# A second decay tile for turned and spread chunks in place of the fifth h tile, with sums three chunks behind

## The chip, the cores and the metric

The kernel runs on one core of one Trainium2 chip. Its time is the device time of one execution in microseconds. All numbers are float32.

## The reference

The kernel computes a conditioned block with two state-space scans, one forward in time and one backward (cut to what matters):

```python
B, S, D, E, N, R = (4, 1024, 512, 1024, 16, 64)
dbc = einsum('bse,re->bsr', u, Wdbc);  dlt, Bm, Cm = split(dbc, [R, R + N])
delta = softplus(einsum('bsr,er->bse', dlt, Wdt) + bdt)
dA = exp(delta[..., None] * -exp(Alog))          # decays, one per state n
dBu = delta[..., None] * Bm[:, :, None, :] * u[..., None]   # inflows
h = dA_t * h + dBu_t                             # scan over the tokens
y = einsum('ben,bn->be', h, C_t)                 # summed over the 16 states
...
y1 = silu(mx) * ssm(z1);  y2 = silu(mx) * flip(ssm(flip(z2)))
out = einsum('bse,de->bsd', y1 + y2, Wf) + bf + skip
return x + gate * out
```

`u` is z1 or z2, a projection of the normalised and modulated input. Batch, direction and channels are independent of each other. Only the scan is serial in time.

## The kernel before

A set-up part (about 250 us) normalises x, folds weights together and writes the projected dlt, B and C rows to DRAM. Then `ssm_kernel` works through 64 **units** (`NU`): 4 batches, 2 directions, 8 tiles of 128 channels. In units 0 to 7 of each sixteen the scan runs forward, in 8 to 15 backward. A unit has 16 **chunks** (c, from 0 to 15), one for each state n, and each chunk is a tile of 128 channels by 1024 tokens. q = 16 k + c numbers the chunks of the whole kernel. All engines run through the same two loops (k, then c), each in its own written order, and meet at semaphores.

A chunk takes these steps:

- ScalarE (ACT) makes the decays, exp(delta * A), at L1195.
- The inflows delta * u * B are made in one of three ways, which the letter of the chunk in `KINDS` names. For **V** and **P** chunks GpSimd (POOL) multiplies du by a broadcast row of B (L1233, tile `bst`) and the decays go to a PSUM tile, `slot[q % 2]`. For **A** chunks (turned) ACT scales the transposed du, eight tiles of 128x128 in two halves of four (`scale_half`, L1134, tile `abuf`), and TensorE (PE) transposes them back into `slot[q % 2]` (`turn_inflow`, L899). For **E** chunks (spread) PE multiplies the transposed du, `dut`, by diagonal matrices of B (`spread_inflow`, L911, two passes per matmul); ACT makes those matrices once in eight units (`make_diagonal`). For A and E the decays go to an SBUF tile, `dec`, of which there is one.
- VectorE (DVE) scans (L1325) into `hbuf[q % HR]` or, for V, into the slot in place.
- The scan is multiplied by a row of C: by DVE for V (L1330), by POOL for all others (`product`, L1238), in place in `hbuf`.
- PE sums the 16 products in PSUM tile `y` by transposing each into it, eight matmuls per chunk (`sum_chunk`, L888).

`HR` is the number of h tiles, `LAG` how many chunks behind its own step PE sums. In step q PE makes the inflow of chunk q, if it is A or E, and then the sum of chunk q - LAG:

```python
def sum_chunk(q):
    wait_product(pe, q)
...
if q >= HR:
    dve.wait_ge(summed, q - HR + 1)      # DVE, before scan q
```

Once per unit, around the border, come these: ACT copies y out (`copy_y`, L1125), then PE starts y anew with the skip terms (`skip_terms`, L881; it waits for that copy) and makes the delta product of the next unit (`delta_product`, L848). ACT turns that into softplus (L1090 to L1096), DVE finishes delta (L1259), PE projects z for the next unit (`z_part`, L859), DVE makes du in two halves (L1269), PE transposes them (`turn_du`, L930), and ACT copies them to `dut` (L1159).

Half of the units (1 to 8 of each sixteen) also compute the silu branch, **mx**: two banks of matmuls, each in two halves (`mx_part`, L869), the last half bank in step 0 of the next unit, ACT's sigmoid on each bank (L1109 to L1117), and a product of DVE (L1279). The other half (9 to 15 and 0) **gate** y: PE transposes it, DVE multiplies (L1291), and from unit 16 on PE projects a block of tokens through Wf (`project`, L969 and L974, half of it in step 15 and half in step 0 of the next unit), which DVE finishes (L1295). Units 9 to 14 have, in that place, the dlt, B and C products of later chunks (L962). In `z_step` the work for z starts at chunk 7 or, in gating units, 9.

POOL's order in each unit, from chunk 6 on, is: products 6 and 7, inflow 11, product 8, inflow 13, products 10 and 11, inflow 15, products 12 and 13, inflow 1 of the next unit, product 14, inflow 3, product 0, inflow 5, product 2, inflow 7, product 4, inflow 9.

Of the kernel before, what the change touches and what calls it, by code (L numbers as in the profile page):

```python
# [27 lines left out]
def setup_kernel(nc, t, scratch):  # L28

    with ExitStack() as ctx:  # L30
# [358 lines left out]
        def _(pe):  # L389
# [93 lines left out]
            for c in range(2):  # L483
# [3 lines left out]
KINDS = "EVEVAVAPAVAPAPAV"  # L487
SCALE_STEPS = {0: (4, 0), 2: (4, 1), 3: (6, 0), 5: (6, 1), 6: (8, 0), 7: (8, 1),
               8: (10, 0), 9: (10, 1), 10: (12, 0), 11: (12, 1), 12: (14, 0), 13: (14, 1)}
SPREAD = [n for n in range(N) if KINDS[n] == "E"]  # L490
SEQ = ET * N
HR = 5
LAG = 4
# [30 lines left out]
def ssm_kernel(nc, t, scratch):  # L524

    with ExitStack() as ctx:
# [3 lines left out]
        def sem(name):  # L530
# [7 lines left out]
        soft, ud, yrd, silu, ybuf, dec, dut = (sb(n, [P, S]) for n in (  # L538
            "soft", "ud", "yrd", "silu", "ybuf", "dec", "dut"))
# [58 lines left out]
        def has_mx(k):  # L598
            return not gates(k) and k % (2 * ET) != 0
# [235 lines left out]
        def _(pe):  # L835
# [183 lines left out]
            for k in range(NU):  # L1019
                e, zs = k % ET, z_step(k)  # L1020
                new_b = (k + 1) % ET == 0
                for c in range(N):
# [5 lines left out]
                    if c == 3 and k + 1 < NU:  # L1028
                        delta_product(k + 1)
                    if c == LAG:  # L1030
                        skip_terms(k)
                    if q >= LAG:
                        sum_chunk(q - LAG)
                    if c == 0 and k > 0 and has_mx(k - 1):
                        mx_part(k - 1, 1, range(2, DT))
# [45 lines left out]
        def _(act):  # L1081
# [71 lines left out]
            def copy_dut(k, h):  # L1153
                act.wait_ge(dut_mm, 2 * k + h + 1)
                if k > 0:
                    act.wait_ge(turned, before("AE", (k - 1) * N + SPREAD[-1] + 1))
                if k > 0:
                    act.wait_ge(scaled, len(SCALE_STEPS) * k - 1 + h)
                nc.scalar.activation(dut[:, half(h)], mb[h], ACT.Copy).then_inc(dut_ready, 1)  # L1159
# [10 lines left out]
            copy_bt(0)  # L1170
            for h in range(2):
                skip_half(0, h)
            for h in range(2):
                copy_dut(0, h)
            for i in range(len(SPREAD)):
                make_diagonal(0, i)

            for k in range(NU):
                f, zs = wtile(k), z_step(k)
                new_b = (k + 1) % ET == 0  # L1180
                for c in range(N):
# [3 lines left out]
                    if kind(q) in "AE":  # L1185
                        if before("AE", q) > 0:
                            act.wait_ge(scanned, TURNED[before("AE", q) - 1] + 1)
                        decays = dec[:]
# [8 lines left out]
                    if c == 0 and k > 0 and k % ET == 0:  # L1197
                        make_diagonal(k // ET, 1)
                    if c in SCALE_STEPS:
                        scale_half(N * k + SCALE_STEPS[c][0], SCALE_STEPS[c][1])  # L1200
# [4 lines left out]
                    if c == LAG - 1 and k > 0:  # L1205
                        copy_y(k - 1)
# [47 lines left out]
        def _(dve):  # L1254
# [55 lines left out]
            for k in range(NU):  # L1310
                zs = z_step(k)
                step = -1 if backward(k) else 1
                for c in range(N):
                    q = N * k + c
                    dve.wait_ge(decay_ready, q + 1)
                    if kind(q) in "AE":
                        dve.wait_ge(turned, before("AE", q + 1))
                        decays, inflows = dec, slot[q % 2]
# [107 lines left out]
```

## Time and profile before

| | |
|---|---|
| median of 3 runs | 3330.06 us (3326.39 to 3333.35) |
| the profiled execution | 3326.98 us |
| its span, first to last instruction | 3325.2 us |
| TensorE busy | 3021.0 us, 91% |
| VectorE busy | 3027.8 us, 91% |
| ScalarE busy | 2681.0 us, 81% |
| GpSimd busy | 2906.2 us, 87% |
| scans (VectorE, L1325) | 1024, 2264 to 2278 ns each |
| products (GpSimd, L1238) | 704, 2383 ns each |
| sums (TensorE, L888) | 8192 transposes |

The span is what the timelines below cover, and their times count from its start. Two instructions of one engine overlap by about 0.1 us in the records, so what an instruction takes of its engine's time is read from the start of one to the start of the next.

### The profile page before, as it was taken

Reading aid. Unit: us, or ns where it says so; the run is one execution under the profiler, and the core shown is the slowest. Engines: PE = TensorE matmul, PEld = TensorE weight load, DVE = VectorE, ACT = ScalarE, POOL = GpSimd, SP = SyncE. Lnnn points to the kernel's source line nnn. Section 1 sums busy time; section 2 is a strip of 40 time slices with the busy share of each in tenths; the row PEclk is TensorE's granted clock in tenths of the full one; section 3 lists DMA queues with packets and bytes.
Section 4 is the critical chain, followed back from the end, with each engine's and each line's share of the span. In section 5 each row is a group of like instructions: output and inputs, shape, how many; then the busy total and the mean of one; then the engine's idle time right before and its main releaser. Section 6 shows DMA issues by size and latency. Waiting matters only on the chain.

```text
span 3325.2 us, 54883 instructions
## 1 busy us (share of the span) xinstructions
PE 3021.0 (91%) x19924; PEld 2416.6 (73%) x19924; DVE 3027.8 (91%) x2008; ACT 2681.0 (81%) x5151; POOL 2906.2 (87%) x1288
## 2 busy tenths in 40 slices
PE   8887999889989999889999999899988989898999
PEld 5766667667767667678878776678777766677789
DVE  2829999999999999999999999999998999999994
ACT  1438999988788999987788999987877999988772
POOL 1518999999999999999998999999998999999993
PEclk9989999999999999999999999999999999999999
DMA  5765333644475343644575333645565344645453
GB/s 222 245 232 173 129 133 127 230 161 148 160 247 190 132 130 126 224 148 151 158 236 188 130 122 135 219 138 163 161 212 202 123 133 129 229 138 163 150 194 112
DMA packets 207054, 560.40 MB, mean 169 GB/s; under 512 B 20201, under 2 KB 66473, under 8 KB 202561
## 3 DMA queue, kind: packets, MB, share of 16 engines
q1 hardware_dynamic: 203424, 538.01, 48.6%
q0 software_dynamic: 2304, 16.78, 1.4%
q8 instruction: 159, 2.61, 0.3%
q10 hardware_dynamic: 1056, 2.10, 0.2%
q14 instruction: 111, 0.90, 0.1%
HBM read 476.19 MB, written 80.63 MB: 167 GB/s over the span
## 4 chain that ended last, share of the span: by engine, by line
PE 56%; ACT 20%; issue 8%; DVE 8%; POOL 1%; DVEq 0%; ACTq 0%; POOLq 0%
PE y L888 17%; PE slot L899 8%; PE mb L859 8%; ACT abuf L1134 7%; PE mb L969 6%; PE mb L869 5%; PE slot L911 5%; DVE hbuf L1325 4%; ACT dec L1195 4%; ACT slot L1195 3%; ACT soft L1090 2%; PE mb L848 2%; DVE slot L1325 2%; PE mb L962 1%; DVE delta L1259 1%
## 5 line engine op out<-in xcount | busy, mean ns | idle before, releaser
L1238 POOL TENSOR_TENSOR hbuf<-hbuf,cres 128x1024 f32<-128x1024 f32 x704 | 1666.6, 2383 | 182.9 <-DVE hbuf L1325 182.3
L1233 POOL TENSOR_TENSOR bst<-bst,du 128x1024 f32<-128x1024 f32 x512 | 1226.6, 2396 | 47.0 <-DVE du L1269 47.0
L1325 DVE TENSOR_TENSOR_SCAN hbuf<-dec,slot 128x1024 f32<-128x1024 f32 x512 | 1165.1, 2276 | 60.5 <-PE slot L911 36.8
L888 PEld LDWEIGHTS y<-ident,hbuf 128*128 128x128 f32 x8192 | 971.6, 146 | 137.9 <-issue 134.2
L888 PE MATMUL y<-ident,hbuf 128*128 128x128 f32 x8192 | 1067.9, 280 | 0.7 <-POOL hbuf L1238 0.7
L1134 ACT ACTIVATE abuf<-dut,bt 128x128 f32<-128x128 f32 x3072 | 970.9, 387 | 0.0
L1325 DVE TENSOR_TENSOR_SCAN slot<-slot,bst 128x1024 f32<-128x1024 f32 x320 | 729.0, 2278 | 43.6 <-ACT slot L1195 43.3
L1195 ACT ACTIVATE dec<-delta,par 128x1024 f32<-128x1024 f32 x512 | 584.7, 1142 | 127.3 <-DVE hbuf L1325 127.3
L1195 ACT ACTIVATE slot<-delta,par 128x1024 f32<-128x1024 f32 x512 | 566.5, 1107 | 118.5 <-DVE hbuf L1330 106.2
L899 PE MATMUL slot<-ident,abuf 128*128 128x128 f32 x3072 | 422.7, 282 | 168.1 <-ACT abuf L1134 148.2
L899 PEld LDWEIGHTS slot<-ident,abuf 128*128 128x128 f32 x3072 | 351.8, 145 | 298.8 <-ACT abuf L1134 223.5
L859 PE MATMUL mb<-xn,wzs 128*128 128x512 f32 x1008 | 478.7, 597 | 25.5 <-DVE delta L1259 15.0
L1325 DVE TENSOR_TENSOR_SCAN hbuf<-slot,bst 128x1024 f32<-128x1024 f32 x192 | 434.7, 2264 | 0.2 <-ACT slot L1195 0.2
L1330 DVE TENSOR_TENSOR hbuf<-slot,cres 128x1024 f32<-128x1024 f32 x320 | 391.9, 1225 | 11.0
L859 PEld LDWEIGHTS mb<-xn,wzs 128*128 128x128 f32 x1008 | 172.8, 191 | 156.2 <-issue 156.2
L911 PEld LDWEIGHTS slot<-diag,dut 128*128 128x128 f32 x2048 | 244.8, 194 | 30.5 <-issue 27.8
L911 PE MATMUL slot<-diag,dut 128*128 128x128 f32 x2048 | 253.6, 278 | 10.5 <-DVE hbuf L1325 5.1
L869 PE MATMUL mb<-xn,wx 128*128 128x512 f32 x512 | 240.9, 593 | 0.0
L969 PE MATMUL mb<-ybuf,wf 128*128 128x128 f32 x1504 | 177.8, 276 | 4.7 <-issue 3.8
L969 PEld LDWEIGHTS mb<-ybuf,wf 128*128 128x128 f32 x1504 | 173.2, 193 | 5.4 <-issue 4.4
L848 PE MATMUL mb<-dl,wdt 81*128 81x512 f32 x256 | 125.2, 610 | 13.7 <-DVE silu L1279 8.4
L1125 ACT ACTIVATE yrd<-y 128x1024 f32<-128x1024 f32 x64 | 64.8, 1013 | 84.1 <-PE y L888 84.0
(157 smaller groups left out, 2322.4 us busy)
## 6 DMA issues: line engine op xcount, KB each, us to landing
bst<-bc_s SPq DMA_DIRECT2D x512, 512.0 KB, 3.9
cres<-bc_s SPq DMA_DIRECT2D x128, 512.0 KB, 6.9
wzs<-wz_s SPq DMA_DIRECT2D x64, 256.0 KB, 4.1
yf_s<-yrd SPq DMA_DIRECT2D x32, 512.0 KB, 5.3
ybuf<-yf_s SPq DMA_DIRECT2D x32, 512.0 KB, 5.0
yg_s<-ybuf SPq DMA_DIRECT2D x31, 512.0 KB, 4.4
si_s<-silu SPq DMA_DIRECT2D x28, 512.0 KB, 6.1
silu<-si_s SPq DMA_DIRECT2D x28, 512.0 KB, 5.4
```

Source lines behind the costliest of these rows:

```text
L859: last = nc.tensor.matmul(z_bank(k, h), wz[:, i * P:(i + 1) * P], xn[:, h, i, :], start=(i == 0), stop=(i == DT - 1))
L869: last = nc.tensor.matmul(mb[h], wx[:, i * P:(i + 1) * P], xn[:, h, i, :], start=(i == 0), stop=(i == DT - 1))
L888: last = nc.tensor.matmul(y[:, j * P:(j + 1) * P], hbuf[:, q % HR, j * P:(j + 1) * P], ident[:], start=False, stop=(q % N == N - 1), is_tr ...
L899: last = nc.tensor.matmul(slot[q % 2][:, j * P:(j + 1) * P], abuf[:, a % 2, j * P:(j + 1) * P], ident[:], start=True, stop=True, is_transp ...
L911: last = nc.tensor.matmul(slot[q % 2][:, j * P:(j + 1) * P], dut[:, j * P:(j + 1) * P], diag[:, i, j, :], start=True, stop=True)
L969: nc.tensor.matmul(bank[:, m * P:(m + 1) * P], wf[:, e, m * P:(m + 1) * P], tokens, start=(e == 0 and m == 0), stop=False, skip_group_chec ...
L1134: last = nc.scalar.activation(abuf[:, a % 2, j * P:(j + 1) * P], dut[:, j * P:(j + 1) * P], ACT.Copy, scale=bt[:, g % 2, j, n:n + 1])
L1195: nc.scalar.activation(decays, delta[:, k % 2, :], ACT.Exp, scale=par[:, f // ET, f % ET, PA + c:PA + c + 1]).then_inc(decay_ready, 1)
L1233: nc.gpsimd.tensor_tensor(bst[:, i % BR, :], bst[:, i % BR, :], du[:, k % 2, :], ALU.mult).then_inc(pool_b, 1)
L1238: nc.gpsimd.tensor_tensor(hbuf[:, q % HR, :], hbuf[:, q % HR, :], cres[:, q % N, :], ALU.mult).then_inc(pool_prod, 1)
L1325: nc.vector.tensor_tensor_scan(h[:, ::step], decays[:, ::step], inflows[:, ::step], 0.0, ALU.mult, ALU.add).then_inc(scanned, 1)
L1330: nc.vector.tensor_tensor(hbuf[:, q % HR, :], slot[q % 2][:], cres[:, c, :], ALU.mult).then_inc(dve_prod, 1)
```

## The change

- Chunks 2 and 4 change places in `KINDS`: 2 is now turned, 4 is spread. ACT scales both halves for chunk 2 in its step 0.
- `dec` becomes two tiles. The decays of the i-th A or E chunk wait for the scan of the one two before it, not for the last.
- `HR` goes from 5 to 4 and `LAG` from 4 to 3. The memory of one h tile is the memory of the second `dec` tile.
- PE's step 3 now has the skip terms, sum 0 and then the delta product; before it had the delta product and sum 15 of the last unit, and the skip terms came in step 4, behind the turned inflow of chunk 4.
- ACT copies y straight behind decay 3, ahead of its scaling. The second diagonal of a new group of eight units is made in step 1 instead of 0.

```diff
-KINDS = "EVEVAVAPAVAPAPAV"
-SCALE_STEPS = {0: (4, 0), 2: (4, 1), 3: (6, 0), 5: (6, 1), 6: (8, 0), 7: (8, 1),
...
+KINDS = "EVAVEVAPAVAPAPAV"
+SCALE_STEPS = {0: ((2, 0), (2, 1)), 3: ((6, 0),), 5: ((6, 1),), 6: ((8, 0),), 7: ((8, 1),), 8: ((10, 0),),
...
-HR = 5
-LAG = 4
+HR = 4
+LAG = 3
+DEC = 2
...
+        dec = sb("dec", [P, DEC, S])
...
-                    if c == 3 and k + 1 < NU:
-                        delta_product(k + 1)
                     if c == LAG:
                         skip_terms(k)
                     if q >= LAG:
                         sum_chunk(q - LAG)
+                    if c == 3 and k + 1 < NU:
+                        delta_product(k + 1)
...
                     if kind(q) in "AE":
-                        if before("AE", q) > 0:
-                            act.wait_ge(scanned, TURNED[before("AE", q) - 1] + 1)
-                        decays = dec[:]
+                        i = before("AE", q)
+                        if i >= DEC:
+                            act.wait_ge(scanned, TURNED[i - DEC] + 1)
+                        decays = dec[:, i % DEC, :]
...
-                    if c == 0 and k > 0 and k % ET == 0:
+                    if c == LAG and k > 0:
+                        copy_y(k - 1)
+                    if c == 1 and k > 0 and k % ET == 0:
                         make_diagonal(k // ET, 1)
                     if c in SCALE_STEPS:
-                        scale_half(N * k + SCALE_STEPS[c][0], SCALE_STEPS[c][1])
+                        for n, h in SCALE_STEPS[c]:
+                            scale_half(N * k + n, h)
...
-                    if c == LAG - 1 and k > 0:
-                        copy_y(k - 1)
```

The numbers of the changed kernel's lines are one or two higher. The order of its instructions at a border with mx on PE, from the sum that stands in step 15 to the scan inflow of chunk 4 (`y<-ident,hbuf` x8 is the sum of one chunk, `y<-ident,ud` are the skip terms, `mb<-dl,wdt` is the delta product). Before:

```order
L888 MATMUL y<-ident,hbuf 128x128 x8
L869 MATMUL mb<-xn,wx 128x512 x2
L911 MATMUL slot<-diag,dut 128x128 x8
L888 MATMUL y<-ident,hbuf 128x128 x8
L869 MATMUL mb<-xn,wx 128x512 x2
L888 MATMUL y<-ident,hbuf 128x128 x8
L911 MATMUL slot<-diag,dut 128x128 x8
L888 MATMUL y<-ident,hbuf 128x128 x8
L848 MATMUL mb<-dl,wdt 128x512 x2
L888 MATMUL y<-ident,hbuf 128x128 x8
L899 MATMUL slot<-ident,abuf 128x128 x8
L881 MATMUL y<-ident,ud 128x128 x8
```

The change:

```order
L889 MATMUL y<-ident,hbuf 128x128 x8
L870 MATMUL mb<-xn,wx 128x512 x2
L912 MATMUL slot<-diag,dut 128x128 x8
L889 MATMUL y<-ident,hbuf 128x128 x8
L870 MATMUL mb<-xn,wx 128x512 x2
L889 MATMUL y<-ident,hbuf 128x128 x8
L900 MATMUL slot<-ident,abuf 128x128 x8
L889 MATMUL y<-ident,hbuf 128x128 x8
L882 MATMUL y<-ident,ud 128x128 x8
L889 MATMUL y<-ident,hbuf 128x128 x8
L849 MATMUL mb<-dl,wdt 128x512 x2
L912 MATMUL slot<-diag,dut 128x128 x8
```

The first sum is of chunk 11 before and of chunk 12 now, and every later one is likewise a chunk further. The turned inflow comes two sums earlier, as chunk 2's; the spread inflow of chunk 4 now stands behind the skip terms, a sum and the delta product.

On ACT at the same border, from decay 0 to the copy of y (`dec` and `slot` are decays 0, 1, 2 and 3, `abuf` x4 is the scaling of one half, `soft` the sigmoid on the second mx bank). Before:

```order
L1195 ACTIVATE dec<-delta,par 128x1024
L1134 ACTIVATE abuf<-dut,bt 128x128 x4
L1195 ACTIVATE slot<-delta,par 128x1024
L1109 ACTIVATE soft<-mb,par 128x512
L1112 ACTIVATE soft<-soft 128x512
L1114 ACTIVATE soft<-soft 128x512
L1117 ACTIVATE soft<-soft 128x512
L1195 ACTIVATE dec<-delta,par 128x1024
L1134 ACTIVATE abuf<-dut,bt 128x128 x4
L1195 ACTIVATE slot<-delta,par 128x1024
L1134 ACTIVATE abuf<-dut,bt 128x128 x4
L1125 ACTIVATE yrd<-y 128x1024
```

The change:

```order
L1197 ACTIVATE dec<-delta,par 128x1024
L1135 ACTIVATE abuf<-dut,bt 128x128 x8
L1197 ACTIVATE slot<-delta,par 128x1024
L1110 ACTIVATE soft<-mb,par 128x512
L1113 ACTIVATE soft<-soft 128x512
L1115 ACTIVATE soft<-soft 128x512
L1118 ACTIVATE soft<-soft 128x512
L1197 ACTIVATE dec<-delta,par 128x1024
L1197 ACTIVATE slot<-delta,par 128x1024
L1126 ACTIVATE yrd<-y 128x1024
L1135 ACTIVATE abuf<-dut,bt 128x128 x4
```

The scaling that stood behind decays 0 and 2 is all behind decay 0, and the copy of y is no longer behind the scaling for chunk 6. On DVE and POOL the order of the instructions is the same, since V, P and the two others keep their places but for 2 and 4, which both take a decay tile and a slot.

## Rows read from the trace of the kernel before

**Rows 1.** the page's first part: busy time and share of each engine

```profile
PE 3021.0 (91%) x19924; PEld 2416.6 (73%) x19924; DVE 3027.8 (91%) x2008; ACT 2681.0 (81%) x5151; POOL 2906.2 (87%) x1288
```

**Rows 2.** waits of DVE: us in total, times, longest

```profile
DVE slot L1325 <- ACT slot L1195: 43.3, 69, 1.7
DVE hbuf L1325 <- PE slot L911: 36.8, 36, 7.5
...
DVE hbuf L1325 <- ACT slot L1195: 17.2, 23, 1.1
```

**Rows 3.** timeline of DVE, units 21 and 22: start us, us, instruction, idle before

```profile
1202.90 2.27 DVE L1325 TENSOR_TENSOR_SCAN hbuf<-dec,slot 128x1024 f32<-128x1024 f32 x1
...
1229.33 2.29 DVE L1325 TENSOR_TENSOR_SCAN hbuf<-dec,slot 128x1024 f32<-128x1024 f32 x1
...
1241.28 2.28 DVE L1325 TENSOR_TENSOR_SCAN hbuf<-dec,slot 128x1024 f32<-128x1024 f32 x1
1243.94 2.30 DVE L1325 TENSOR_TENSOR_SCAN slot<-slot,bst 128x1024 f32<-128x1024 f32 x1 [0.39 <-ACT slot L1195]
...
1248.55 2.28 DVE L1325 TENSOR_TENSOR_SCAN hbuf<-dec,slot 128x1024 f32<-128x1024 f32 x1
```

**Rows 4.** timeline of POOL, the same stretch

```profile
1205.32 4.69 POOL L1238 TENSOR_TENSOR hbuf<-hbuf,cres 128x1024 f32<-128x1024 f32 x2 [1.43 <-DVE hbuf L1325]
...
1223.89 4.78 POOL L1238 TENSOR_TENSOR hbuf<-hbuf,cres 128x1024 f32<-128x1024 f32 x2
```

**Rows 5.** timeline of PE (matmuls), the same border

```profile
1225.57 1.88 PE L869 MATMUL mb<-xn,wx 128*128 128x512 f32 x4
1227.29 1.95 PE L911 MATMUL slot<-diag,dut 128*128 128x128 f32 x16
...
1229.95 1.88 PE L869 MATMUL mb<-xn,wx 128*128 128x512 f32 x4
...
1240.01 1.07 PE L881 MATMUL y<-ident,ud 128*128 128x128 f32 x8 [0.89 <-ACT yrd L1125]
...
1245.16 1.09 PE L899 MATMUL slot<-ident,abuf 128*128 128x128 f32 x8 [2.34 <-ACT abuf L1134]
1246.10 3.37 PE L888 MATMUL y<-ident,hbuf 128*128 128x128 f32 x16
```

**Rows 6.** timeline of ACT, the same border

```profile
1231.87 0.69 ACT L1109 ACTIVATE soft<-mb,par 128x512 f32<-128x512 f32 x1 [1.08 <-PE mb L869]
...
1234.45 1.14 ACT L1195 ACTIVATE dec<-delta,par 128x1024 f32<-128x1024 f32 x1
...
1238.87 1.00 ACT L1125 ACTIVATE yrd<-y 128x1024 f32<-128x1024 f32 x1
```

**Rows 7.** timeline of DVE, border of units 28 and 29

```profile
1607.26 2.29 DVE L1325 TENSOR_TENSOR_SCAN hbuf<-dec,slot 128x1024 f32<-128x1024 f32 x1 [0.56 <-PE slot L911]
...
1614.80 2.29 DVE L1325 TENSOR_TENSOR_SCAN hbuf<-dec,slot 128x1024 f32<-128x1024 f32 x1 [0.77 <-ACT slot L1195]
...
1620.46 2.27 DVE L1325 TENSOR_TENSOR_SCAN hbuf<-dec,slot 128x1024 f32<-128x1024 f32 x1
1623.32 2.30 DVE L1325 TENSOR_TENSOR_SCAN slot<-slot,bst 128x1024 f32<-128x1024 f32 x1 [0.59 <-ACT slot L1195]
```

**Rows 8.** timeline of POOL, the same border

```profile
1600.91 4.74 POOL L1238 TENSOR_TENSOR hbuf<-hbuf,cres 128x1024 f32<-128x1024 f32 x2
```

**Rows 9.** timeline of PE, the same border

```profile
1599.46 1.91 PE L888 MATMUL y<-ident,hbuf 128*128 128x128 f32 x16
1601.21 0.60 PE L930 MATMUL mb<-ident,du 128*128 128x128 f32 x4
...
1605.22 1.95 PE L911 MATMUL slot<-diag,dut 128*128 128x128 f32 x16
```

**Rows 10.** engines in a stretch: busy PE, PEld, DVE, ACT, POOL, PEclk, DMA, GB/s

```profile
1246.00:1251.00 5.00, 5.00 (x23) 4.04 (x22) 4.96 (x5) 4.62 (x12) 3.62 (x3) 0.66 0.36 121
```

**Rows 11.** cores: span and mean granted clock

```profile
core 0: 3325.2 us, clock 0.975
```

More of the change, by code:

```diff
@@ L484, in _ @@
                 project(1, c, ps[c % 2])
-KINDS = "EVEVAVAPAVAPAPAV"
-SCALE_STEPS = {0: (4, 0), 2: (4, 1), 3: (6, 0), 5: (6, 1), 6: (8, 0), 7: (8, 1),
-               8: (10, 0), 9: (10, 1), 10: (12, 0), 11: (12, 1), 12: (14, 0), 13: (14, 1)}
+KINDS = "EVAVEVAPAVAPAPAV"
+SCALE_STEPS = {0: ((2, 0), (2, 1)), 3: ((6, 0),), 5: ((6, 1),), 6: ((8, 0),), 7: ((8, 1),), 8: ((10, 0),),
+               9: ((10, 1),), 10: ((12, 0),), 11: ((12, 1),), 12: ((14, 0),), 13: ((14, 1),)}
 SPREAD = [n for n in range(N) if KINDS[n] == "E"]
 SEQ = ET * N
-HR = 5
-LAG = 4
+HR = 4
+LAG = 3
+DEC = 2
 DR = 2
@@ L537, in ssm_kernel @@
         delta, du = (sb(n, [P, 2, S]) for n in ("delta", "du"))
-        soft, ud, yrd, silu, ybuf, dec, dut = (sb(n, [P, S]) for n in (
-            "soft", "ud", "yrd", "silu", "ybuf", "dec", "dut"))
+        soft, ud, yrd, silu, ybuf, dut = (sb(n, [P, S]) for n in ("soft", "ud", "yrd", "silu", "ybuf", "dut"))
+        dec = sb("dec", [P, DEC, S])
         abuf = sb("abuf", [P, 2, S])
@@ L1157, in copy_dut @@
                 if k > 0:
-                    act.wait_ge(scaled, len(SCALE_STEPS) * k - 1 + h)
+                    act.wait_ge(scaled, 2 * KINDS.count("A") * k - 1 + h)
                 nc.scalar.activation(dut[:, half(h)], mb[h], ACT.Copy).then_inc(dut_ready, 1)
@@ L1170, in _ @@
             copy_bt(0)
+            make_diagonal(0, 0)
             for h in range(2):
@@ L1174, in _ @@
                 copy_dut(0, h)
-            for i in range(len(SPREAD)):
-                make_diagonal(0, i)
+            make_diagonal(0, 1)
             for k in range(NU):
@@ L1317, in _ @@
                         dve.wait_ge(turned, before("AE", q + 1))
-                        decays, inflows = dec, slot[q % 2]
+                        decays, inflows = dec[:, before("AE", q) % DEC, :], slot[q % 2]
                     else:
```

## Prediction

> **What bounds the kernel now.** I read the page first: VectorE (DVE) is busy for 91% of the span, and GpSimd (POOL) for 87% [rows 1]. Both times are in large equal pieces, so the next question is which of them waits, and for whom. The waits of DVE answer it: its two largest causes in the units are the decay factors of ScalarE (ACT) and the inflows of TensorE (PE), 97 us in all with the third row [rows 2]. No row of that view is a wait for a sum of PE. So DVE sets the pace, nearly packed, and a change can win 97 us at most by taking waits of DVE away. It can lose without such a ceiling, if it puts something late in front of DVE.
>
> The timelines show what is close behind. I take two borders between units, since the 64 units repeat them. Scan c means the scan of chunk c of a unit, and a prime is the next unit. The first border is between units 21 and 22, which have the silu branch (mx). Scan 6 starts at 1202.90 and one period later at 1248.55: 45.65 us [rows 3]. POOL picks up product 6 as soon as scan 6 is over (1205.32, after a wait of 1.43), and from there it never waits until the next product 6. In its fixed order (products 6, 7, inflow 11, product 8, inflow 13, products 10, 11, inflow 15, product 12) it reaches **product 12** nine operations later: the pair 12 and 13 starts at 1223.89, so product 12 is ready at about 1226.25 [rows 4]. That is 21 us after scan 6, in which DVE has come eight scans further, to scan 14. PE asks for that product only after the spread inflow of chunk 0', and does not wait [rows 5]. **This lag of POOL at the end of a unit is what the old distance of four chunks hides.**
>
> **The change, part by part.**
>
> *Sums three behind (LAG 4 to 3).* PE runs in order. In step 15 of a unit it now sums chunk 12 where it summed 11, and behind that sum stand the first mx half of the second bank and the spread inflow that scan 0' needs. PE finished the previous sum and began that mx half at 1225.57, so it asked at 1224.70 (a sum of eight transposes takes 0.87: sixteen take 1.75, from 1599.46 to 1601.21). Now it must wait to 1226.25. With 0.1 us for the signal: sum to 1227.22, mx half 1.72 (1225.57 to 1227.29) to 1228.94, and scan 0' starts 2.04 after its spread begins (1227.29 to 1229.33) [rows 3, 5]: 1230.97 in place of 1229.33, **+1.64**. Step 13 has the same for product 10, but only about 0.4 late at scan 14, and what follows swallows it.
>
> Units without mx (gating ones) have the stretch of PE from 1599.46 on: sums 10 and 11, a turn of du, half of a projection, the spread inflow at 1605.22 [rows 9]. Sum 11 begins there at 1600.33. Product 12 is the first of the pair that starts at 1600.91 [rows 8] and is ready at 1603.25, so sum 12 starts at 1603.35 in that place and everything behind it is 3.0 later: scan 0' at 1610.3, not 1607.26 [rows 7], **+3.0**. 32 units end the first way, and 29 the second (23 with a projection, 6 with the products for the next pair of chunks, which I count alike). Units 0 and 15 have nothing behind that sum and lose nothing. 32 x 1.64 + 29 x 3.0 = **+139 us**.
>
> *h tiles 5 to 4.* Scan q now needs sum q-4. PE makes it in step q-1, as it made q-5 before, so the condition is no tighter than the PE order just costed. Sum 14 is the nearest: product 14 ends three POOL operations, about 7.0 us, after product 12, so 2.3 us after the new scan 0', and scan 2' starts only about 6 us after scan 0' (two scans, a product and a silu half of DVE between). Nothing added.
>
> *Chunk 2 turned, chunk 4 spread; skip terms, sum and delta product ahead of it.* Before, PE turned chunk 4 and then waited for ACT's copy of y (0.89 at 1240.01) with nothing urgent behind [rows 5]. Now the skip terms wait for the copy in step 3, and behind them stand sum 0', the delta product and the spread inflow of chunk 4, which scan 4' needs. For the mx border, counted from scan 0': the mx half of PE begins at +0.62 [rows 3, 5], ACT's sigmoid starts at +2.54 and takes 2.58 (1231.87 to 1234.45) [rows 6], then decays 2 and 3 at 1.05 each, to 7.22, the copy, and the skip terms 1.14 after its start (1238.87 to 1240.01): 8.4. Skip terms 0.91, sum 0.87, delta product 1.72 (as many passes as an mx half), and 2.04 from spread to scan: **13.9**. Scan 4' stood at 11.95 (1229.33 to 1241.28) [rows 3]: **+1.95**. Product 0' ends five POOL operations after product 12, at about 6.9, and is in time. At the gating border PE itself sets the copy: from -0.25 it does sum 13 0.87, half a projection 3.58 (4.01 from 1601.21 to 1605.22 less 0.43 for the turn of du [rows 9]), its skip tile 0.44, sum 14, turn 2 and sum 15 at 0.87 each, so the copy starts at about 7.4, the skip terms at 8.55, and scan 4' at **14.1**; it stood at 13.2 (1607.26 to 1620.46) [rows 7], **+0.9**. In it the wait of 0.77 before scan 2' is gone, since a turn (0.87) replaces a spread (1.8). For the 6 units behind a product job I take +1.2, for the two behind neither +2. 32 x 1.95 + 23 x 0.9 + 6 x 1.2 + 2 x 2 = **+94 us**.
>
> *Second decay tile, scaling moved, copy of y ahead of it.* ACT no longer waits for the last scan before a decay of a turned chunk. DVE gains only where ACT was late: scan 5 came 2.66 after scan 4 behind mx units [rows 3] and 2.86 behind gating ones [rows 7]. Unhindered scans follow each other at 2.19 (2.28 less an overlap of 0.09), so 0.47 and 0.67 were lost. Now the softplus start is not queued behind the copy, and decay 5 is ready about 1 us early. 31 x 0.47 + 29 x 0.67 = **-34 us**. At the seven borders where B changes, ACT also makes diagonals and DVE waits for its slot up to 1.7 us [rows 2]; that hides partly under the new waits: **-4**. The scaling of chunk 2 (2.4 us) comes after decay 0' and is ready before PE's turn; no instruction and no DMA is added. SP's queue has the same order; its wait for the copy of y moves with the unit.
>
> The sum without the clock is 139 + 94 - 34 - 4 = **+195 us**.
>
> *TensorE's clock.* After a wait of 2.34 at 1245.16, the next sixteen transposes took 3.37 us [rows 5], 1.46 more than the 1.91 of the same shape [rows 9], and from 1246 to 1251 the granted clock was 0.66 of full speed [rows 10]: the lower level, 1.2 GHz, for 3.4 us (0.34 x 5 / 0.5), and 2.4 GHz for the rest. This is off the path now. After the change PE waits about 2.9 before sum 12 in gating units and about 3.2 before the skip terms in mx units, and both times the work behind leads straight to a scan. 61 such waits could cost 1.46 each, 89 us, or nothing. Were every unit to lose one such stretch now (3.4 us at half speed in 46), the mean clock would be 0.963; it is 0.975 [rows 11], two thirds of that. I take two thirds: **+60 us**.
>
> The Trainium skill, page "TensorE: Matmul & The Clock Gate", Part 1, says that the array's clock goes to its lower level when the engine has been idle and comes back only with sustained activity. That speaks against this change: by that rule every one of the longer waits is followed by a slow stretch, and the sum is 195 + 89. By [rows 10] the trace agrees for the one wait that I looked at closely.
>
> Sum: 3327 us of the profiled execution (span 3325.2 and 1.8 around it) + 255 = **3582 us**. That execution is 3 us below the median of the runs, 3330, which is under my error.
>
> **Rivals.**
> *Both waits, each followed by the low clock.* 3327 + 195 + 89 = 3611. For it: the wait of 2.34 is already followed by it, and the new ones are longer. Against: it could begin too late to touch the path. With the forecast it shares the mechanism.
>
> *One of the two new waits only.* If the chain to scan 4' is shorter than I add up (it runs through three engines), +139 - 34 - 4 - 22 (the waits before scan 2') gives 3406. If product 12 were in time, +94 - 38 gives 3383. Against the latter is the pair at 1223.89, whose start is bound to the end of scan 6 by POOL's nine operations.
>
> *Faster, by ACT.* If PE's sums were not late, DVE would be rid of its waits in the units: 0.39 in 31 of them [rows 3], 1.92 in 29 (0.56 + 0.77 + 0.59 [rows 7]), and some 7 us at the borders where B changes, 75 us in all: 3252. For it: all of those waits name ACT or PE's inflows [rows 2], and these are what the second tile and the swap relieve. It decides only if product 12 is ready within about 0.1 us of the time when PE reaches step 15, that is 1.6 us sooner in mx units and 3 us sooner in gating ones. POOL, 2.33 us an operation without a gap, gives no sign of that.
>
> *Nothing.* Gains and losses equal, 3320 to 3337. Only by chance.
>
> **How the numbers follow.** Forecast (3480 to 3640, likeliest 3582) 0.68; the full clock rule 0.12, inside the same range; one wait only 0.12; faster 0.06; nothing 0.02. The range 3460 to 3640 holds the first two whole. Its low end is the sum without the clock and with half of the chunk 4 term missing (3327 + 148 = 3475) and 15 us for my rounding; its high end is 3611 and half a microsecond per unit of waits that I overlooked. A measurement here can tell about 0.2%, 7 us. Faster 0.06, same 0.02, slower 0.92.
>
> **What would show it.** Right: PE waits for "POOL hbuf" before sums, some 60 times, about 1 to 3 us each (no row here has one); PE's wait for "ACT yrd" grows from 0.89 in mx units to about 3; DVE waits for "PE slot" at scans 0 and 4, its waits for "ACT slot" at scan 5 are gone; periods of about 49 to 51 us for mx units and 51 to 53 for gating ones; the mean clock is at or below 0.975. Wrong: periods under 46.5 in mx units, or a DVE wait for anything else that is larger.

## The result, and the profile after

The changed kernel takes 3575.57 us (median of 4 runs, 3574.32 to 3580.31), the kernel before 3331.22 (median of 4). The ratio is 1.0738, with a 95% interval of 1.072 to 1.0757: the change costs 244 us (248 between the two executions that the profiles show, of 3326.98 and 3574.61). The forecast was 3582, range 3460 to 3640, slower at 0.92.

The same work is done in more time. First the page's line of busy times, which answers to [rows 1]:

```profile
PE 3059.3 (86%) x19924; PEld 2399.7 (67%) x19924; DVE 3028.8 (85%) x2008; ACT 2681.1 (75%) x5151; POOL 2904.9 (81%) x1288
```

DVE, ACT and POOL are as busy as before within 2 us, and every share has fallen. PE has 38 us more; no matmul was added, and at least part of it is work that now falls into stretches of the lower clock (below). So nearly all of the loss is waiting, and as DVE set the pace, it must be in front of DVE. Its waits, by what ended them (us in total, times, longest), answer to [rows 2]:

```profile
DVE hbuf L1328 <- PE slot L912: 267.6, 91, 5.2
DVE hbuf L1328 <- issue: 46.2, 56, 1.7
...
DVE slot L1328 <- ACT slot L1197: 10.9, 12, 1.3
```

The waits for ACT's decays in `slot`, 43.3 us before, are down to 10.9. In their place DVE waits 268 us for the spread inflow, the one of chunk 0 or of chunk 4, where it waited 37. The row "issue", for which the profile names no releaser, is PE's inflow too: it is 28 waits before scan 0 of 1.05 us and 27 before scan 14 of 0.56, and scan 0 starts there 2.04 us after PE began the spread inflow (1368.06 and 1370.10 below), as it does where PE is named (1333.14 and 1335.18). What PE in turn waited for (the same view of PE; before, it had 0.7 us of the first row and 35.2 of the second):

```profile
PE y L889 <- POOL hbuf L1241: 162.3, 222, 3.2
PE y L882 <- ACT yrd L1126: 152.5, 62, 5.7
```

These are the two mechanisms of the forecast, though not all of each row: only 64 of the 222 waits for POOL are over 1 us, some 30 of about 1.3 (sum 10, in step 13 of mx units) and 28 of about 2.3 (sum 12, in step 15 of gating ones). Adding up from DVE's timeline what it was idle before each scan, by chunk, over the units 1 to 62 and the first chunks of 63, gives this table (us; "mx" are the 32 units that come behind an mx unit, "gating" the others):

| before scan | mx, before | mx, after | gating, before | gating, after |
|---|---|---|---|---|
| 0 | 0 | 29 | 22 | 118 |
| 1 and 2 | 7 | 3 | 27 | 4 |
| 4 | 0 | 99 | 0 | 59 |
| 5 | 12 | 0 | 16 | 0 |
| 14 | 0 | 16 | 0 | 2 |
| 15 | 6 | 4 | 3 | 4 |
| all | 25 | 151 | 69 | 186 |

That is 337 us after and 93 before, a difference of 244. There are some 46 more waits than before, and each costs the overlap of 0.1 us as well, so that this is the whole of the 248 between the two profiled executions.

**The border behind an mx unit.** DVE's timeline of unit 21 of the changed kernel (start, us, instruction, idle before) answers to [rows 3]:

```profile
1319.63 2.29 DVE L1328 TENSOR_TENSOR_SCAN hbuf<-dec,slot 128x1024 f32<-128x1024 f32 x1 [1.05 <-issue]
...
1335.18 2.29 DVE L1328 TENSOR_TENSOR_SCAN hbuf<-dec,slot 128x1024 f32<-128x1024 f32 x1 [3.51 <-PE slot L912]
1337.38 2.27 DVE L1328 TENSOR_TENSOR_SCAN slot<-slot,bst 128x1024 f32<-128x1024 f32 x1
...
1362.66 2.29 DVE L1328 TENSOR_TENSOR_SCAN hbuf<-dec,slot 128x1024 f32<-128x1024 f32 x1 [0.56 <-issue]
...
1370.10 2.29 DVE L1328 TENSOR_TENSOR_SCAN hbuf<-dec,slot 128x1024 f32<-128x1024 f32 x1 [1.05 <-issue]
```

and PE's of the same stretch answers to [rows 5]:

```profile
1327.98 1.59 PE L882 MATMUL y<-ident,ud 128*128 128x128 f32 x8 [3.21 <-ACT yrd L1126]
1329.36 1.91 PE L889 MATMUL y<-ident,hbuf 128*128 128x128 f32 x8
1331.06 2.24 PE L849 MATMUL mb<-dl,wdt 81*128 81x512 f32 x4
1333.14 1.95 PE L912 MATMUL slot<-diag,dut 128*128 128x128 f32 x16
...
1358.44 1.09 PE L889 MATMUL y<-ident,hbuf 128*128 128x128 f32 x8 [1.28 <-POOL hbuf L1241]
...
1365.41 1.09 PE L889 MATMUL y<-ident,hbuf 128*128 128x128 f32 x8 [0.25 <-POOL hbuf L1241]
1366.34 1.88 PE L870 MATMUL mb<-xn,wx 128*128 128x512 f32 x4
1368.06 1.95 PE L912 MATMUL slot<-diag,dut 128*128 128x128 f32 x16
```

In 1327.98 to 1335.18 the chain to scan 4 stands link by link: skip terms, sum 0, delta product, spread inflow, scan. The skip terms start 8.35 us after scan 0 (8.4 in the forecast). With 1327.98 to 1335.18 at 7.2 the chain is 1.65 longer than the 5.54 of the forecast: that is the low clock, seen in the first three rows (to the next row the skip terms take 1.38 and not 0.91, the sum 1.70 and not 0.87, the delta product 2.08 and not 1.72). The two waits for "POOL hbuf" are sums 10 (1.28, step 13) and 12 (0.25, step 15). The wait is split over two places: sum 10 already delays PE, so that little is left for sum 12. Scans 14 and 0 come late by 0.56 and 1.05. What fixes scan 0 is still product 12: from scan 6 (1341.96) to scan 0 it is 28.14 us, and the forecast had 28.07.

**The border behind a gating unit.** PE at the end of unit 28, and DVE's scans 0 and 4 of unit 29, answer to [rows 9] and [rows 7]:

```profile
1724.70 1.09 PE L889 MATMUL y<-ident,hbuf 128*128 128x128 f32 x8 [2.32 <-POOL hbuf L1241]
1725.63 0.60 PE L931 MATMUL mb<-ident,du 128*128 128x128 f32 x4
1726.06 3.74 PE L970 MATMUL mb<-ybuf,wf 128*128 128x128 f32 x32
1729.64 1.95 PE L912 MATMUL slot<-diag,dut 128*128 128x128 f32 x16
```

```profile
1731.68 2.29 DVE L1328 TENSOR_TENSOR_SCAN hbuf<-dec,slot 128x1024 f32<-128x1024 f32 x1 [3.55 <-PE slot L912]
...
1745.83 2.29 DVE L1328 TENSOR_TENSOR_SCAN hbuf<-dec,slot 128x1024 f32<-128x1024 f32 x1 [1.75 <-PE slot L912]
```

Scan 4 is 14.15 us after scan 0; the forecast had 14.1. The pair of products that begins with product 12 starts at 1722.29 on POOL, so sum 12 can start when it does:

```profile
1722.29 4.68 POOL L1241 TENSOR_TENSOR hbuf<-hbuf,cres 128x1024 f32<-128x1024 f32 x2
```

### The profile page after: what moved, and what is told of

It is laid out like the page before. It is cut to its first block, busy times and chain, and to the rows that moved or that the text cites. A ratio compares the mean times of both kernels' runs of the same rounds, so it can differ in the third digit from the quotient of the medians.

```text
span 3572.8 us, 54883 instructions
## 1 busy us (share of the span) xinstructions
PE 3059.3 (86%) x19924; PEld 2399.7 (67%) x19924; DVE 3028.8 (85%) x2008; ACT 2681.1 (75%) x5151; POOL 2904.9 (81%) x1288
## 4 chain that ended last, share of the span: by engine, by line
PE 32%; POOL 28%; issue 13%; ACT 10%; DVE 10%; DVEq 0%; POOLq 0%; ACTq 0%
POOL hbuf L1241 20%; PE y L889 8%; POOL bst L1236 8%; PE mb L970 5%; DVE hbuf L1328 5%; PE slot L912 5%; PE mb L849 4%; PE mb L870 3%; DVE slot L1328 2%; DVE delta L1262 2%; PE y L882 2%; PE slot L900 2%; ACT yrd L1126 2%; ACT slot L1197 2%; ACT abuf L1135 2%
## 5 line engine op out<-in xcount | busy, mean ns | idle before, releaser
L889 PE MATMUL y<-ident,hbuf 128*128 128x128 f32 x8192 | 1087.2, 278 | 162.4 <-POOL hbuf L1241 162.3
L889 PEld LDWEIGHTS y<-ident,hbuf 128*128 128x128 f32 x8192 | 937.2, 143 | 325.6 <-POOL hbuf L1241 288.2
L1328 DVE TENSOR_TENSOR_SCAN slot<-slot,bst 128x1024 f32<-128x1024 f32 x320 | 727.6, 2274 | 10.9 <-ACT slot L1197 10.9
L900 PEld LDWEIGHTS slot<-ident,abuf 128*128 128x128 f32 x3072 | 343.9, 141 | 210.6 <-issue 129.6
L900 PE MATMUL slot<-ident,abuf 128*128 128x128 f32 x3072 | 406.1, 275 | 88.2 <-ACT abuf L1135 62.9
L882 PE MATMUL y<-ident,ud 128*128 128x128 f32 x512 | 77.0, 299 | 152.5 <-ACT yrd L1126 152.5
L1091 ACT ACTIVATE soft<-mb 128x1024 f32<-128x1024 f32 x64 | 65.5, 1024 | 149.2 <-PE mb L849 149.2
```

The lines of the kernel that those rows point to most:

```text
L889: last = nc.tensor.matmul(y[:, j * P:(j + 1) * P], hbuf[:, q % HR, j * P:(j + 1) * P], ident[:], start=False, stop=(q % N == N - 1), is_tr ...
L900: last = nc.tensor.matmul(slot[q % 2][:, j * P:(j + 1) * P], abuf[:, a % 2, j * P:(j + 1) * P], ident[:], start=True, stop=True, is_transp ...
L1328: nc.vector.tensor_tensor_scan(h[:, ::step], decays[:, ::step], inflows[:, ::step], 0.0, ALU.mult, ALU.add).then_inc(scanned, 1)
```

## The experiments

The theory: two sequences on PE are each stalled by a wait in front of work that a scan needs. In step 15 it is sum 12, which waits for POOL; in step 3 it is the skip terms, which wait for ACT's copy. The rivals: it is the number of tiles that binds; or the whole unit is bound by POOL and the waits only show it. Measured beside each group of runs, the kernel before took 3326.2 to 3331.2 us, so differences between groups are good to some 5 us.

### Sum 12 moved to the end of step 15 (late15)

```diff
-                    if q >= LAG:
+                    if q >= LAG and not (c == N - 1):
                         sum_chunk(q - LAG)
...
+                    if q >= LAG and (c == N - 1):
+                        sum_chunk(q - LAG)       # last in step c, behind mx_part or project
```

> The changed kernel, with one sum moved: in step 15 PE sums chunk 12 at the end of the step, behind the mx half or the projection half, instead of at its beginning; everything else stays. Theory (in the trace of the changed kernel PE stands in step 15 until POOL has product 12, and what scan 0 of the next unit needs is queued behind it): the waits of DVE before scan 0 fall from 1.05 to about 0 in 32 units that end with mx and from 3.5 to 5.2 to about 0.5 in 29 gating ones, so about 33 + 107 = 140 us less, 3435 us. The waits before scan 4 and the 0.56 before scan 14 stay. Rival 1 (the four h tiles are what binds, not PE's order): scan 0 still waits, now for the sum itself, and the time stays near 3575. Rival 2 (the whole unit is bound by POOL and the border wait is only where that shows): scan 0 comes earlier, but the time moves into the wait before scan 4, over 3520.

Measured: 3491.7 us, 84 less than the changed kernel. The wait before scan 0 fell from 29 to 16 us in mx units and from 118 to 47 in gating ones, and the 0.56 before scan 14 stayed (16 us). Rival 1 is out, since scan 0 comes 2 us earlier in gating units with four tiles, and rival 2 too, since the wait before scan 4 did not grow (99 to 91, 59 to 58). But the gain was 84 and not 140. In mx units 11 us reappear before scan 1, where decay 1 now stands behind both halves of chunk 2's scaling. In gating units 1.40 is left before scan 0, not 0.5: the 0.56 of the kernel before, and 0.87 for sum 12, which has only moved to just in front of the spread inflow, as four h tiles demand. In mx units PE still waits 1.2 us for sum 10 in step 13, and that is what is left before scans 14 and 0 there.

### The delta product ahead of the skip terms (delta_first)

```diff
+                    if c == 3 and k + 1 < NU:
+                        delta_product(k + 1)
                     if c == LAG:
                         skip_terms(k)
                     if q >= LAG:
                         sum_chunk(q - LAG)
-                    if c == 3 and k + 1 < NU:
-                        delta_product(k + 1)
```

> The changed kernel, with the delta product back ahead of the skip terms in step 3, so that PE makes it while it waits for the copy of y; everything else stays. Theory (skip terms, sum 0, delta product and spread inflow stand in a row behind ACT's copy, and the wait of 3.2 us in front of them brings the lower clock): scan 4 comes at about 12.2 us after scan 0 in mx units and 12.8 in gating ones, its waits fall from 3.1 on average and 1.8 to about 0.3 each, 32 x 2.8 + 29 x 1.4 = 132 us less, 3443 us. Waits before scan 0 stay. Rival (the spread inflow alone is late, because it takes 1.8 us where a turn takes 0.9): only the 1.72 us of the delta product are won, or less, and the clock still falls, about 3575 - 61 x 1.0 = 3515.

Measured: 3471.9 us, 104 less. The waits before scan 4 fell from 99 to 24 us and from 59 to 12, those before scan 0 in gating units rose from 118 to 133, since 18 of them are now over 5 us where 9 were (the lower clock, below). The gain lies between the theory's 132 and the rival's 60, closer to the first. Of the 24 that stay 8 are in units 8, 24, 40 and 56, where ACT's diagonals come in between. The others are nine waits of 1.8 us, and they too are the lower clock: from scan 0 to scan 4 the granted clock is 0.88 in such a unit (20) and 1.00 in one without the wait (19).

### The spread inflow of chunk 4 ahead of the skip terms, the delta product behind (spread4)

```diff
-                    elif kind(q) == "E":
+                    elif kind(q) == "E" and c == 0:
                         spread_inflow(q)
+                    if c == 3:
+                        spread_inflow(q + 1)
```

> The changed kernel, with the spread inflow of chunk 4 moved to the head of step 3, ahead of the skip terms; the delta product stays behind them. Theory (not only the inflow but also the delta product is on the path, through softplus, which stands ahead of decay 5 on ACT): scan 4 loses its wait for the inflow, but the delta product ends later, at about 13.8 us after scan 0, decay 5 at 17.0, and scan 5 then waits some 2.5 us for ACT; scan 5 comes about where it came before, so 3575 within 40 us. Rival (the late inflow of chunk 4 is the whole of the second loss): its waits vanish and nothing takes their place, 3575 - 99 - 52 = about 3425 us.

Measured: 3711.2 us, 136 **more** than the changed kernel. Its waits of DVE:

```profile
DVE slot L1330 <- ACT slot L1199: 172.5, 75, 2.6
DVE hbuf L1330 <- PE slot L912: 109.3, 25, 5.6
DVE hbuf L1330 <- PE y L889: 104.3, 64, 3.6
```

The rival is out by far: the late inflow of chunk 4 is not the whole of it. What the theory named is there, a wait of 2.5 us before scan 5 for decay 5, which stands behind softplus and so behind the delta product (159 us before scan 5). Its sum was still wrong, because it left out the third row: with four h tiles scan 4 also needs sum 0, and PE reaches that sum only behind the inflow (1.8 us), the copy and the skip terms. Scan 4 waits on (102 us in all), now for the sum. Here the four tiles themselves bind.

### Both corrections (late_delta), and the sums of steps 13 and 14 moved too (late13_delta)

The second replaces `c == N - 1` in the first diff by `c >= 13`.

> The changed kernel with both corrections: sum 12 at the end of step 15, and the delta product ahead of the skip terms. Theory (two separate losses that add up): 3575 - 140 - 132 = 3303 us, below the kernel before (3331), since the waits of DVE before scans 2 and 5 that the second decay tile took away stay away. Rival (the two losses overlap, or a third limit, POOL's 44.3 us of work in each unit, stands right behind): 3331 or more.

> As the kernel with both corrections, but the sums of steps 13 and 14 (chunks 10 and 11) also stand at the end of their step, as that of step 15. Theory (what is left of the loss, 0.57 before scans 0 and 14, 0.38 before scan 1 in mx units and 1.4 before scan 0 in gating ones, is the same wait for POOL in two earlier steps; PE still waits 106 us for POOL there): 3371 - 32 x 1.5 - 29 x 0.9 = 3297 us, about 1% below the kernel before. Rival (POOL's own 44.3 us of work in a unit is the limit now, and its lag grows as DVE gets faster): the waits move to scans 1 and 3, which wait for POOL's inflows, and the time stays over 3350.

Measured: 3371.1 us and 3341.3 us. The first is 204 below the changed kernel, more than 84 + 104 = 188, so the two losses are separate; the slow stretches that delta_first had are nearly gone too (no wait before scan 0 is over 2.6 us). The forecasts of 3303 and 3297 were both too low, mostly by what was left before scans 0, 1 and 14 in the first and before scan 0 of gating units in the second. In the second kernel the waits before scans 0 and 14 in mx units are gone (of the 151 us of all waits in mx units 28 are left), but there is a new one before scan 15 in most of these units, of 0.35 us, and it is for a sum of PE:

```profile
1232.00 2.27 DVE L1330 TENSOR_TENSOR_SCAN hbuf<-dec,slot 128x1024 f32<-128x1024 f32 x1
1234.62 2.30 DVE L1330 TENSOR_TENSOR_SCAN slot<-slot,bst 128x1024 f32<-128x1024 f32 x1 [0.35 <-PE y L889]
```

Scan 15 waits for sum 11, which now stands at the end of step 14. In gating units the 1.40 before scan 0 did not move at all; PE's timeline there has no wait from the turn of du on:

```profile
1612.72 0.66 PE L931 MATMUL mb<-ident,du 128*128 128x128 f32 x4
1613.21 3.74 PE L970 MATMUL mb<-ybuf,wf 128*128 128x128 f32 x32
1616.78 1.04 PE L889 MATMUL y<-ident,hbuf 128*128 128x128 f32 x8
1617.65 1.95 PE L912 MATMUL slot<-diag,dut 128*128 128x128 f32 x16
```

So with four tiles a sum is either ahead of urgent work and waits for POOL, or behind it and late for a scan. This is the furthest repaired of the kernels here with four tiles, and it is still at 1.004 of the kernel before (interval 1.0025 to 1.0055). Other places for these sums were not tried.

### One decay tile instead of two (late13_delta_dec1)

```diff
-DEC = 2
+DEC = 1
```

> As the kernel with the sums of steps 13 to 15 late and the delta product first, but with one decay tile instead of two (the decays of a turned or spread chunk wait for the scan of the last one again). It measures what the second tile is worth where the sums are not in the way. Theory (ACT has slack in most of a unit, and the tile is only worth the waits at the border, where scaling and sigmoid stand behind decay 0): 20 to 60 us slower than the same kernel with two tiles, so about 3337. Rival (the tile is worth nothing, the gain came from the moved scaling and copy of y): the same time within 7 us.

Measured: 3344.0 us, against 3341.3 with two tiles, measured side by side; 1.0051 (1.0036 to 1.0066) against 1.004 (1.0025 to 1.0055) of the kernel before. The rival is right: there the second decay tile is worth nothing that this shows. ACT's 127 us of waits for the one `dec` tile, in the kernel before, were idle time of an engine with 20% to spare.

### The kernel before, with sum 12 in step 15 (before_early12)

```diff
-                    if q >= LAG:
+                    if q >= LAG and not (c == 0 and k > 0):
                         sum_chunk(q - LAG)
+                    if c == N - 1 and k + 1 < NU:
+                        sum_chunk(q - LAG + 1)
```

> The kernel before (five h tiles, four behind, one decay tile, its order of chunks), with one sum moved: PE sums chunk 12 in step 15, behind chunk 11, instead of in step 0 of the next unit. Theory (the wait for product 12 in step 15 is by itself the first loss, whatever the number of tiles): scan 0 comes 1.64 us later in 32 units and 3.0 later, with some of the lower clock, in 29, so 3329 + 52 + 95 = about 3475 us. Rival (five tiles give the room, so that only the change as a whole brings the wait): 3329 within 15 us.

Measured: 3436.2 us, ratio 1.034 (1.0315 to 1.0365), 110 us slower. Moving one sum of eight transposes across a border costs 110 us in a kernel that is otherwise untouched, with five tiles. The wait before scan 0 rose from 0 to 49 us in the mx units (1.5 each) and from 22 to 121 in the gating ones (3.4 each), about as forecast; of the 147 us forecast 37 did not come, because the forecast did not give back the waits that the later start hides (35 us before scans 2 and 5).

### The changed kernel with the tiles of the kernel before (tiles_of_before)

```diff
-HR = 4
+HR = 5
 LAG = 3
-DEC = 2
+DEC = 1
```

> The changed kernel with the tiles of the kernel before: five h tiles and one decay tile, but sums three behind and all its orders. Theory (the loss is in what PE has queued behind its waits, and neither the number of h tiles nor the second decay tile has a part in it): 3575 us within 15. Rival (the four h tiles cost part of it, or the second decay tile wins part of it back): 15 us or more away from 3575, below or above.

Measured: 3577.5 us, the changed kernel's 3575.6 within 2. So the loss is in the order and in the distance of three; the exchange of a tile, which gives the change its name, does nothing to the time as long as these stay. This run changes both numbers of tiles at once. That the fifth h tile and the second decay tile do not just cancel is seen in the waits: no scan of the changed kernel waits for a sum, and the table above is the same within 6 us in each of its two sums (155 and 180 for 151 and 186).

### Filling PE's wait (filler)

```diff
+                    if c == LAG and k + 1 < NU and k > 0 and has_mx(k - 1):
+                        delta_product(k + 1, filler=True)   # the same two matmuls, no signal
                     if c == LAG:
                         skip_terms(k)
```

> The changed kernel, with the two matmuls of the delta product made once more ahead of the skip terms in step 3 of the units behind an mx unit, without a signal; the delta product itself stays where the change put it, so the path has the same work, and PE only waits 1.5 us instead of 3.2 for the copy of y. Theory (the wait before scan 4 is 1.84 at the full clock, and 3.5 or 5.2 in 20 of 32 units because the clock falls to 1.2 GHz after the long wait): all 32 waits are about 1.84, 40 us less in all, 3535 us. Rival (the long waits before scan 4 have another cause, or the clock falls whatever PE does there): 3575, or more by what the added matmuls delay.

Measured: 3550.0 us, 26 less, although PE has more to do. Of the 32 waits before scan 4 in these units 21 are now of 1.81 to 1.86 us, where 12 were; their sum is 79 us, was 99. So the clock is part of the long waits, but the filler takes away only 20 of the 40 us of waits that I ascribed to it. PE's own waits for the copy fell from 152 to 63 us, and 23 us of waits in front of the filler came in.

### The order of the chunks alone, with five tiles (five_tiles_copy_late, five_tiles)

Both keep `KINDS` and `SCALE_STEPS` of the change, with

```diff
-HR = 4
-LAG = 3
-DEC = 2
+HR = 5
+LAG = 4
+DEC = 1
```

and the delta product ahead of the sum in step 3. In the first ACT copies y behind its other work of step 3, in the second straight behind decay 3, as in the change.

> Built from the changed kernel: chunk 2 turned, chunk 4 spread, both halves scaled behind decay 0, but five h tiles, four behind and one decay tile as before, the delta product ahead of the sum in step 3, and the copy of y behind the scaling as before. Theory (four tiles force a sum, 0.87 us, in front of scan 0 in gating units, and the second decay tile is worth nothing there, so the order of the chunks is the only part of the change that wins): the wait of 0.77 before scan 2 goes in 29 gating units, those of 0.56 before scan 0 and about 0.5 before scan 5 stay: 3329 - 25 = 3304 us. Rival (the wait before scan 2 only moves on to scan 4, whose spread inflow takes 0.9 us more than a turn): the time of the kernel before, within 7 us.

> The same with the copy of y ahead of the scaling, as the change has it. Theory (with sums four behind, PE reaches sum 15 only 9.8 us after scan 0 in gating units, so ACT stands before the copy with the scaling queued behind it, and decay 5 comes at about 16.2 for a scan that could start at 14.6; in mx units the 0.4 before scan 5 goes): 3304 + 29 x 1.1 - 32 x 0.4 = 3323 us. Rival (the copy ahead of the scaling wins as it stands in the changed kernel): below 3304.

Measured: 3303.5 us (0.9922, interval 0.9908 to 0.9937) and 3361.1 us (1.0097, interval 1.0082 to 1.0112). The first is the fastest kernel here, 26 us below the kernel before on the same chip, where 25 were forecast. DVE at the border of units 28 and 29 of it, against [rows 7]:

```profile
1601.41 2.29 DVE L1328 TENSOR_TENSOR_SCAN hbuf<-dec,slot 128x1024 f32<-128x1024 f32 x1 [0.56 <-PE slot L912]
...
1608.10 2.28 DVE L1328 TENSOR_TENSOR_SCAN hbuf<-dec,slot 128x1024 f32<-128x1024 f32 x1
...
1613.74 2.28 DVE L1328 TENSOR_TENSOR_SCAN hbuf<-dec,slot 128x1024 f32<-128x1024 f32 x1
1616.56 2.30 DVE L1328 TENSOR_TENSOR_SCAN slot<-slot,bst 128x1024 f32<-128x1024 f32 x1 [0.55 <-ACT slot L1197]
```

The wait before scan 2 is gone, the one before scan 0 is what it was, and scan 4 is in time, since its spread inflow stands ahead of the skip terms again. Two things were not in the forecast: in mx units the waits before scan 5 went as well (12 us to 1), and those before scan 1 grew (7 to 13), behind the scaling of both halves.

The second shows what the copy of y costs when it stands ahead of the scaling without being available. ACT in unit 28:

```profile
1582.69 1.12 ACT L1197 ACTIVATE slot<-delta,par 128x1024 f32<-128x1024 f32 x1 [2.30 <-DVE hbuf L1333]
1586.96 1.02 ACT L1126 ACTIVATE yrd<-y 128x1024 f32<-128x1024 f32 x1 [3.15 <-PE y L889]
1587.88 1.27 ACT L1135 ACTIVATE abuf<-dut,bt 128x128 f32<-128x128 f32 x4
1589.05 1.14 ACT L1197 ACTIVATE dec<-delta,par 128x1024 f32<-128x1024 f32 x1
```

ACT stands 3.15 us before the copy with the scaling and decay 4 queued behind it. The direction was forecast, not the size: 58 us instead of 19, since decay 4 is late too (29 us before scan 4, where 3 were), and in mx units 17 us come in before scan 5, where a gain was forecast.

## Why the prediction was right

Measured 3575.6 against 3582. The steps of the forecast, one by one:

- **What bounds**: DVE, and a wait in front of it costs its full length. Shown: the idle time before scans grew by 244 us and the profiled execution by 248, with some 4 for the number of waits.
- **Sums three behind**, +1.64 and +3.0 a unit. Measured from the table, mx units lose 29 + 16 us before scans 0 and 14, some 51 with the 0.1 that DVE needs after each wait, against 52. Gating ones lose 96 before scan 0, of which 15 is the clock, against 87. That product 12 is what PE waits for was shown by moving that sum alone, in both kernels (-84 and +110). "What follows swallows it", said of sum 10, was half right: in mx units PE stands 1.3 us at sum 10 and only 0.25 at sum 12, and sum 10 had to be moved as well before the mx units lost their waits.
- **h tiles 5 to 4: nothing added.** Right for the changed kernel (no scan waits for a sum; 3577.5 with five and one decay tile). It is not free in general: scans wait for sums in three of the runs with other orders (104 us in spread4, 10 in each of the late13 kernels), and with sum 12 late it stands 0.87 us in front of scan 0 of gating units.
- **Chunk 4**, +1.95 and +0.9. The chain came link by link: skip terms at 8.35 (8.4), scan 4 at 14.15 in gating units (14.1). The waits without the clock are 32 x 1.84 = 59 us in mx units against 62, and 59 less the 23 before scan 2 in gating ones against 32.
- **Second decay tile, moved scaling and copy**, -34. The waits before scan 5 that went were 28 us as recorded, 34 with the 0.1 for each. The tile's own part is nil within the error, as the run with one tile showed. In mx units the moved scaling is enough, for in five_tiles_copy_late these waits went with one tile and the copy where it had been. In gating ones 15 us stayed there, and what takes them away in the changed kernel, the copy behind decay 3 or the later scan 4, is not shown.
- **Borders where B changes**, -4: about right for the seven together, but not for the reason given. From scan 8 of one unit to scan 8 of the next, the four behind mx units lost 4.7 us each where other such borders lost 4.2, because the diagonals of step 1 now stand ahead of the sigmoid and the copy (PE waits 5.7 us for the copy there, and not 3.2). The three behind gating units lost 1.1 on average where others lost 3.9. DVE had waited there before, 5.7 us before scan 0 of unit 48 alone.
- **Clock**, +60 as two thirds of 89. From the waits: nine of the waits before scan 0 in gating units are of 5.1 to 5.2 us where most others are of 3.4 to 3.6, some 15 us; in mx units, without the four where B changes, the waits before scan 4 are 81 us and would be 51 at 1.84 each, some 30 us. Together 45. Counted by units, 9 of 29 waits of the first kind and 16 of 28 of the second have a slow stretch behind them, 25 of 57. So the two thirds, taken from the mean clock, were too many, and the sum came as close as it did partly by luck. The filler run took away 18 of the 30 us.

The rival with a slow stretch behind every long wait gave 3611: the lower clock came after some of the equal waits and not after others. So the rule of the Trainium skill (page "TensorE: Matmul & The Clock Gate", Part 1), read as the forecast read it, for each single wait, overstates the loss here. The sum without the clock, 3522, is 54 too low, of which 45 are the clock.

Of the signs named beforehand, the waits of DVE at scans 0 and 4, the end of those at scan 5, PE's wait of 3.2 for the copy and the periods (48.8 to 52.1 and 51.4 to 53.0 us) came, and no other wait of DVE in the units is larger. Two were off: PE waits for POOL 222 times and not some 60, if 64 times over 1 us, and the mean clock is 0.976, not at or below 0.975.

## What to carry to other kernels

When an engine runs in order, put each of its waits as late in the step as the consumers of what it waits for allow. One sum of 0.9 us, asked for one step earlier, cost 110 us here, since 4 to 6 us of urgent work stood behind it. Before a distance between producer and consumer is cut, read from the timeline how far the producer lags where it lags most (POOL at the end of a unit, not on average), and set a tile more or less against that. Waits of an engine with slack (ACT's 127 us for the decay tile) are no reason to give it memory that the pacing engine's ring uses.

## What the runs showed of the hardware that was not expected

Two waits of PE of equal length, in the same place of the program, are followed by different clocks. In units 28 and 27 of the changed kernel PE waits 2.32 and 2.33 us before sum 12, and the same 32 matmuls behind take 3.74 us in the one and 5.36 us in the other (the first is shown above, from 1726.06):

```profile
1671.70 1.09 PE L889 MATMUL y<-ident,hbuf 128*128 128x128 f32 x8 [2.33 <-POOL hbuf L1241]
1672.63 0.60 PE L931 MATMUL mb<-ident,du 128*128 128x128 f32 x4
1673.07 5.36 PE L970 MATMUL mb<-ybuf,wf 128*128 128x128 f32 x32
```

The wait of DVE before scan 0 is 3.55 us in the one and 5.18 in the other. So the periods of most units come in steps: 48.8, 50.5 and 52.1 us for mx units, 51.4 and 53.0 for gating ones, a step being 1.6 to 1.7 us. In delta_first the lower clock came in unit 20 where PE had waited only 0.49 and then 0.76 us, and not in unit 19, with waits of 0.48 and 0.76 (granted clock 0.88 and 1.00 from scan 0 to scan 4). In the stretch behind the wait of 3.21 before the skip terms of unit 21, the granted clock was 0.68 of full speed, between 1.2 and 2.4 GHz (last columns: clock, DMA share, GB/s):

```profile
1327.90:1333.20 5.30, 5.22 (x21) 4.09 (x22) 3.74 (x3) 2.14 (x5) 5.30 (x3) 0.68 0.34 80
```

The mean granted clock hides this: 0.976 here and 0.975 before [rows 11]. By that mean the lower stretches took as large a share before, but they lay beside the path: the periods behind mx units were then 45.65 to 45.75 us, but for the borders where B changes.
